# Attention pipeline on one core: full-array pieces and weighings in alternate slots, one double bank for the maxima

## What is computed

```python
def _L0_attn_ref(x, Wqkv, bqkv, Wout, bout):        # 16 heads of 8
    qkv = (x @ Wqkv + bqkv).reshape(B, S, 3, NUM_HEADS, HEAD_DIM)
    q, k, v = (qkv[0] * SCALE, qkv[1], qkv[2])      # after a transpose
    attn = jax.nn.softmax(jnp.einsum('bhqd,bhkd->bhqk', q, k), axis=-1)
    out = jnp.einsum('bhqk,bhkd->bhqd', attn, v)    # back to (B, S, D)
    return out @ Wout + bout

def step(c, xt):                                    # over the 16 images, in _L0_ffn_ref
    ft = jax.nn.sigmoid(xt @ wf.T + c @ uf.T + bf)
    it = jax.nn.sigmoid(xt @ wi.T + c @ ui.T + bi)
    gt = jnp.tanh(xt @ wc.T + c @ uc.T + bc)
    return ft * c + it * gt, None

x = x + _L0_attn_ref(_layernorm(x), ...)
x = x + _L0_ffn_ref(_layernorm(x), ...)
```

## Time and profile before

| what | us |
|---|---|
| median of the runs (three) | 636.96 |
| lowest and highest run | 636.06 and 641.02 |
| span of the profiled execution | 592.2 |
| its own time, taken at the median of the runs, so around the span | 44.8 |
| TensorE busy in the span | 490.3 (83%) |
| vector engine busy | 415.1 (70%) |
| ACT busy | 346.6 (59%) |
| GpSimd busy | 364.7 (62%) |

### The profile page before, as it was taken

One profiled execution on the slowest core, in us unless ns is written; L12 is line 12 of the kernel. 1 busy time (PEld: TensorE's weight loads), 2 busy tenths in 40 slices (PEclk: granted clock), 3 DMA queues, 4 the chain that ended last, 5 costly groups with the idle time before them and its releaser, 6 DMA issues. The chain is left out here.

```text
span 592.2 us, 14069 instructions
## 1 busy us (share of the span) xinstructions
PE 490.3 (83%) x4162; PEld 331.7 (56%) x4162; DVE 415.1 (70%) x1041; ACT 346.6 (59%) x749; POOL 364.7 (62%) x602
## 2 busy tenths in 40 slices
PE   4757889999999999998886899998657999888900
PEld 3423455555555555554463666666547898887800
DVE  6767878888888888784244899999856685454306
ACT  2026767777777777767723678887641565554500
POOL 3555677777777777534324158888764477777740
PEclk8769999999999999999999999998958899999955
DMA  3666435433343444210009999999921333333229
GB/s 106 166 170 190 128 87 128 109 85 101 98 105 110 110 112 109 83 36 4 2 2 317 379 376 365 367 366 366 329 63 53 93 86 96 95 90 89 76 80 353
DMA packets 78750, 90.00 MB, mean 152 GB/s; under 512 B 8395, under 2 KB 56032, under 8 KB 78688
## 3 DMA queue, kind: packets, MB, share of 16 engines
q1 hardware_dynamic: 72824, 79.67, 44.9%
q0 software_dynamic: 4576, 8.47, 4.3%
q10 hardware_dynamic: 1288, 1.11, 0.7%
HBM read 30.47 MB, written 59.72 MB: 152 GB/s over the span
## 5 line engine op out<-in xcount | busy, mean ns | idle before, releaser
L456 DVE TENSOR_REDUCE negmax<-p_dve 128x4 f32<-128x1024 f32 x128 | 156.2, 1223 | 46.9 <-PE p_dve L682 45.2
L574 ACT ACTIVATE probs<-p_exp 128x1024 f32<-128x1024 f32 x128 | 130.7, 1021 | 29.6 <-PE p_exp L656 28.8
L1606 POOL DMA_INDIRECT back<-XN2T,rows x79 | 82.6, 1045 | 36.8 <-issue 21.3
L1114 POOL DMA_INDIRECT disp<-pay,pos x64 | 65.3, 1021 | 18.1 <-issue 18.1
L673 PE MATMUL p_out<-probs,V 128*32 128x256 f32 x1024 | 75.2, 388 | 0.0
L656 PE MATMUL p_exp<-QS,KS 64*128 64x256 bf16 x512 | 50.6, 276 | 11.1 <-ACT probs L574 5.9
L682 PE MATMUL p_dve<-KS,QS 61*128 61x256 bf16 x512 | 51.2, 280 | 9.8 <-DVE negmax L456 9.7
L1731 ACT ACTIVATE hid<-p_qkv,own 128x128 f32<-128x128 f32 x150 | 42.8, 369 | 15.7 <-PE p_qkv L1769 15.4
L1661 DVE TENSOR_SCALAR own<-expert,every_bit 128x578 int32 x79 | 39.8, 545 | 8.4 <-issue 8.4
L1769 PE MATMUL p_qkv<-XN2T,own 128*128 128x128 f32 x316 | 43.2, 279 | 0.8 <-ACT XN2T L1705 0.8
L1122 POOL TENSOR_TENSOR roots<-roots,power 128x4 f32<-128x4 f32 x19 | 25.8, 1358 | 29.2 <-DVE roots L1318 28.7
(11 more groups left out here) (272 smaller groups left out, 1186.0 us busy)
## 6 DMA issues: line engine op xcount, KB each, us to landing
disp<-fill SPq DMA_DIRECT2D x8, 4160.0 KB, 38.1
scratch<-part SPq DMA_DIRECT2D x32, 192.0 KB, 2.1
KS<-scratch SPq DMA_DIRECT2D x32, 192.0 KB, 3.2
QS<-scratch SPq DMA_DIRECT2D x32, 192.0 KB, 4.3
rows<-disp SPq DMA_DIRECT2D x79, 65.0 KB, 1.8
scratch<-part SPq DMA_DIRECT2D x32, 128.0 KB, 1.9
own<-back SPq DMA_DIRECT2D x8, 512.0 KB, 6.9
expert<-in_W_dram SPq DMA_DIRECT2D x1, 2064.0 KB, 8.8
```

Source lines behind the costliest of these rows:

```text
L456: dve.tensor_reduce(negmax[q][:, i, :, 2 * hp:2 * hp + 2], p_dve[buf][:, :].rearrange("p (v w k) -> p v w k", v=HALF, k=S), AX.X, ALU.max, ...
L574: act.activation(probs[s % 4][:, :, :, :].rearrange("p v w q -> p (v w q)"), p_exp[:, :], ACT.Exp)\
L1114: pool.indirect_dma_start(out=disp, out_offset=bass.IndirectOffsetOnAxis(ap=pos[q][:, i, k:k + 1], axis=0), in_=pay[q][:, k, i, :], in_off ...
L1606: pool.indirect_dma_start(out=back, out_offset=bass.IndirectOffsetOnAxis(ap=rows[r][:, h, D + 1:ROW].bitcast(U32), axis=0), in_=y[r][:, h, :],
```

## The change

It does these things:

- Weighings come in pairs in slots 1, 3, 5 and 7 only; the last two of an image move from slot 0 to slot 1 of the next iteration.
- Full-array pieces stand in slots 0, 2, 4 and 6 only, in one function `whole_array`: slot 0 the turn of xn1 and V; slot 2 QK, the turn of the heads for all tokens, the turn of xn2; slot 4 the turn of `on`, the turn of the maxima, the candidate gate; slot 6 the output projection and the two gates.
- PSUM is laid out anew: all maxima go to one double bank `p_max`; the other double bank is cut in two, `p_tok` for V, the heads and the output projection, `p_cell` for xn2 and the candidate gate. Each maxima unit waits for the reduction of the unit before it.
- The vector engine does the quotient for all tokens in one pair of instructions in slot 2 and V's bias in slot 1. In the cell step the two waits change places.
- ACT copies `p_out` in slots 1 and 5, QK in slot 2, xn2 in slot 3, `on` in slot 4, and takes the tanh of the candidate gate in slot 5 and of the two gates in slot 7.

```diff
-WEIGHED_IN = {2: (0,), 3: (1,), 4: (2, 3), 6: (4,), 7: (5,)}
+WEIGHED_IN = {3: (0, 1), 5: (2, 3), 7: (4, 5)}
-DVE_BANK = (0, 1, 1, 1, 1, 0, 1, 1)
...
-        p_dve = [psum(f"p_dve{i}", 1024) for i in range(2)]
+        p_small = psum("p_small", 1024)
+        p_tok, p_cell = p_small[:, 0:512], p_small[:, 512:1024]
+        p_max = psum("p_max", 1024)
...
-                    if s in (1, 2) and active(n, 3):
-                        quotient(n - 3, s - 1)
-                    if s == 3 and active(n, 0):
+                    if s == 2 and active(n, 3):
+                        quotient(n - 3)
+                    if s == 1 and active(n, 0):
...
-                        if s == 4:
-                            copy_out(n - 2, (r - 2) % RING, 0)
-                    if s == 0 and active(n, 3):
-                        copy_out(n - 3, r, 1)
...
+                    if s == 1 and active(n, 3):
+                        copy_out(n - 3, r, 1)
+                    if s == 2 and active(n, -1):
...
+                        if active(n, 1):
+                            act.wait_ge(maxT_p.sem, maxT_p.at(n - 1))
...
+                    if s == 5 and active(n, 2):
+                        copy_out(n - 2, (r - 2) % RING, 0)
+                    if s == (5 if active(n, 2) else 7) and active(n, 4):
+                        b = n - 4
+                        act.wait_ge(gc_p.sem, gc_p.at(b))
+                        if cell.due(b - 1):
+                            act.wait_ge(cell.sem, cell.at(b - 1))
+                        act.activation(carry[:, 1, :], (p_cell if active(n, 2) else p_out)[:, 0:S], ACT.Tanh, bias=gates_b[:, 2:3]).then_inc(gc_s.sem, 1)
+                    if s == (7 if active(n, 2) else 5) and active(n, 4):
...
+            def turn_heads(n, r):
+
+                b = n - 3
+                pe.wait_ge(OT_s.sem, OT_s.at(b))
+                if active(n, 0):
+                    pe.wait_ge(v_s.sem, v_s.at(n))
+                elif active(n, 4):
+                    pe.wait_ge(x1_s.sem, x1_s.at(n - 4))
+                for i in range(TT):
+                    for side in range(SIDES):
+                        first = i * S + side * P
+                        turned_heads = p_tok[:, first:first + P].rearrange("p (l j c) -> p j l c", l=2, j=4)
+                        mm = pe.transpose(turned_heads, OT[r][:, side, i * P:(i + 1) * P], ident[:, :])
+                mm.then_inc(OQ_p.sem, 1)
...
+            def whole_array(n, r, s):
+
+                if s == 0:
                     if active(n, -1):
+                        turn_xn1(n, r)
+                    if active(n, 0):
+                        project_v(n, r)
+                elif s == 2:
+                    if active(n, -1):
+                        project_qk(n, r)
                     if active(n, 3):
+                        turn_heads(n, r)
+                    if active(n, 4):
+                        turn_xn2(n, r)
+                elif s == 4:
+                    if active(n, 3):
+                        turn_on(n, r)
                     if active(n, 1):
+                        turn_max(n)
+                    if active(n, 2) and active(n, 4):
+                        candidate(n, p_cell)
+                    if active(n, 3) and not active(n, 2):
+                        project_out(n, r)
+                elif s == 6:
...
+                    if active(n, 3) and active(n, 2):
+                        project_out(n, r)
+                    if active(n, 4):
+                        two_gates(n)
+                    if active(n, 4) and not active(n, 2):
+                        candidate(n, p_out)
...
-                        bank_free(n, s)
+                        if max_s.due(b, u):
+                            pe.wait_ge(max_s.sem, max_s.at(b, u))
...
-                        maxima(b, q, u, DVE_BANK[s])
-                    if s == 0 and active(n, 3):
+                        maxima(b, q, u)
+                    if s == 1 and active(n, 3):
                         weigh(n - 3, r, 6)
                         weigh(n - 3, r, 7)
...
+                    if s % 2 == 0:
+                        whole_array(n, r, s)
```

More of the change, by code:

```diff
@@ L631, in iteration @@
                                 .then_inc(gfi_s.sem, 1)
-                    if s == 7 and active(n, 4):
-                        b = n - 4
-                        act.wait_ge(gc_p.sem, gc_p.at(b))
-                        act.activation(carry[:, 1, :], (p_misc if active(n, 2) else p_out)[:, 0:S], ACT.Tanh, bias=gates_b[:, 2:3]).then_inc(gc_s.sem, 1)
             def copy_out(b, q, side):
@@ L675, in weigh, with maxima @@
                 mm.then_inc(pv_p.sem, 1)
[L677 removed]
+            def maxima(b, q, u):
                 i, hp = u // 4, u % 4
@@ new lines, in project_out, with candidate @@
+            def project_out(n, r):
+                pe.wait_ge(onT_s.sem, onT_s.at(n - 3))
+                if at(n, 3):
+                    pe.wait_ge(w_in.sem, w_in.at(0))
+                for i in range(TT):
+                    mm = pe.matmul(p_tok[:, i * P:(i + 1) * P], onT[:, i * P:(i + 1) * P], Wout[:, :], start=True, stop=True)
+                mm.then_inc(proj_p.sem, 1)
+            def candidate(n, bank):
+                b = n - 4
+                if cell.due(b - 1):
+                    pe.wait_ge(cell.sem, cell.at(b - 1))
+                else:
+                    pe.wait_ge(setup_done.sem, 4)
+                if active(n, 2):
+                    pe.wait_ge(xn2T_s.sem, xn2T_s.at(b))
+                else:
+                    pe.wait_ge(OT_s.sem, OT_s.at(B - 1))
+                pe.matmul(bank[:, 0:S], gates_w[:, 2, :], xn2T[:, :], start=True, stop=False)
+                pe.matmul(bank[:, 0:S], gates_uh[:, 2, :], state[:, :], start=False, stop=True).then_inc(gc_p.sem, 1)
@@ new lines, in two_gates @@
+            def two_gates(n):
+                b = n - 4
+                if active(n, 1):
+                    pe.wait_ge(maxT_s.sem, maxT_s.at(n - 1))
+                elif active(n, 2):
+                    pe.wait_ge(onT_s.sem, onT_s.at(n - 3))
+                else:
+                    pe.wait_ge(xn2T_s.sem, xn2T_s.at(b))
+                    pe.wait_ge(cell.sem, cell.at(b - 1))
+                for j in range(2):
+                    pe.matmul(p_misc[:, j * S:(j + 1) * S], gates_w[:, j, :], xn2T[:, :], start=True, stop=False)
+                    mm = pe.matmul(p_misc[:, j * S:(j + 1) * S], gates_uh[:, j, :], state[:, :], start=False, stop=True)
+                mm.then_inc(gfi_p.sem, 1)
```

256 lines of the change are left out of this document (87 added, 169 removed).

## The result

The changed kernel takes 645.76 us (median of four runs, 642.63 to 646.84), the kernel before 636.51 in the four runs beside it: ratio 1.0133, 95% interval 1.0082 to 1.0184. I had predicted 637.6 with 630.5 to 643.5. The change makes the kernel slower by 1.3%, and the time lies above the range.

What follows compares the result with a forecast made beforehand. It took TensorE to set the pace, except slots 0 to 2, a vector-engine chain. Fill +1.2, steady part +1.4 and drain -2.0 gave +0.6 on the 636.96 us median: 637.6 us, range 630.5 to 643.5.

Steps and rivals of the forecast that it cites:

- fill: Stretch up to 89 us: +2.6 at the first scores of image 0, net +1.2, bounds -1.5 and +4.
- steady part: Iterations 5 to 14: 16.26 us each instead of 16.12, +1.4 in all, bounds -3.4 and +4.4.
- drain: Last iterations, mostly without maxima: the regrouping pays up to ACT's limit, -2.0 us, bounds -4 and 0.
- it is won back in part: Fill, iterations 2 to 4: earlier maxima (about 0.5 and 0.3 us) and 0.6 more slack bring +2.6 to +1.2.
- the turn of the maxima in slot 4: TensorE, slot 4: about 0.13 us, taken as half a pair of turns because it is bf16.
- The main mechanism: One double bank: maxima wait for the previous reduction, 1.72 us apart in slots 3, 5, 7; slots 0 and 1 3.90.
- rival A: TensorE's switches decide and the single bank costs nothing: 623.1 us, chance 0.07; half of it, 632.8 us, chance 0.14.
- The holds' price: Steady iteration: TensorE's waits for reductions through the single bank cost 1.45 us.
- The cover of the quotient: Vector engine, slot 2: the quotient ends near 2.66, next maxima ready at 2.81, so hidden by 0.15 us.
- rival B: Slot 2's quotient of both halves delays the reduction behind it, 0.6 us per iteration: 643.6 us, chance 0.13.
- TensorE's own order: Steady iteration on TensorE if nobody else is late: 14.81 us, 1.3 below 16.12.
- Rival C: Fill at its upper bound because TensorE's low clock stretches maxima and QK: +2.8, 640.4 us, chance 0.10.

Runs made afterwards that it cites:

- e2: Changed kernel with each reduction reading only half of the keys; 580.03 us, steady iteration 15.21 us.
- e3: Kernel before the change with each reduction reading only half of the keys; 596.44 us, steady iteration 15.93 us.
- e5: Changed kernel with the maxima alternating between two double banks in iterations 0 to 2 only; 604.07 us.
- e6: Changed kernel with the turn of the maxima put first in slot 4; 604.7 us, steady iteration 16.31 us.
- e9: Changed kernel again, unaltered; 644.99 us (median of six), ratio 1.0158 to the kernel before.
- e8: Changed kernel with the edits of e5 and e6, the cell step's second instruction moved to slot 1, slot 7's maxima in the other double bank; 590.27 us.
- e10: Same code as e8, against the kernel before; 630.09 us (median of six), ratio 0.990.
- e1: Kernel before the change again, unaltered; 593.54 us.
- e11: Kernel before the change with only the cell step's second instruction moved to slot 1; 638.08 us (median of twelve), ratio 1.0037.
- e7: Changed kernel with 19 matmuls on the identity added in the last iteration's waits; 608.22 us.

## Why the prediction was wrong

The forecast was +0.6, of three terms: fill +1.2, steady part +1.4, drain -2.0. They measured +5.3, +3.9 and +1.8. The step that failed most is in the fill, "it is won back in part": between the first scores and iteration 5 nothing is won back, 1.5 us more are lost. In the steady part a size was off, the turn of the maxima in slot 4. In the drain a lower clock, for which the sum has no term, took more than the new order gave.

**The main mechanism was right.** The single bank puts TensorE on the vector engine's chain of 1.72 us in slots 0, 5 and 7 and leaves M(0) to M(2) at 3.9. e2 and e3 show it against rival A, which fell: with the chain out of the way the iteration is 15.21, not 16.50. The Trainium skill's rule ("Perfetto Trace Analysis", Optimizing Tensor Performance, Matmuls) that independent matmul groups should rotate through PSUM banks is borne out: e5 gives the fill its second bank back, and from the first maxima to the first scores it takes 21.60 instead of 23.65. The holds' price comes from e2: 1.28 per iteration; I had put it at 1.45.

**Steady part, +1.4 predicted, +3.9 measured.** Slot by slot, predicted and measured: M(0) to M(2) 3.90, 3.91; slot 2 2.38, 2.26; slot 3 1.72, 1.81; slot 4 1.91, 2.20; slots 5, 6, 7 1.72, 2.91, 1.72, then 1.71, 2.93, 1.70. The mis-sized term is slot 4: I took "about 0.13 (half a pair, it is bf16)" for the turn of the maxima, which no row of mine showed. It adds 0.22 for itself and 0.1 in each of the pieces around it, 0.42 in all; e6 took 0.19 of that away by order alone. The cover of the quotient, 0.15 by my sum, was in truth -0.11. It started at M(2) + 1.92 (I had 1.97), but the reduction behind it started only at + 2.79: 0.40 from the start of the reciprocal and 0.47 from that of the product to the next. The maxima of slot 3 could have been reduced at + 2.26 + 0.42. This is rival B in kind, but with 0.09 us for slot 3, not 0.6, and in six of the ten iterations only. TensorE's own order was put at 14.81; e2 shows 15.21. Slot 4 is 0.28 of the difference, slot 0 another 0.23: its turn starts 0.50 behind the maxima there, as I had said, which the 1.72 was to hide and does hide in the changed kernel. Slot 2 gives 0.12 back.

**Fill, +1.2 predicted, +5.3 measured.** This is the largest miss and lies outside its own bounds (-1.5 to +4). Up to the first scores I had +2.6; in e9, whose first maxima start where they did before, it is 44.30 - 41.67 = +2.6. That is luck. Of my 2.6, 0.5 was V ahead of the first maxima, and these start no later in e9 (20.66 against 20.67). The chain behind them costs 2.65 (23.65 against 21.00) where I had 2.1. "1.72 to 1.9 each" was too short: at the low clock it is 1.93 from the fifth unit on. And the count that matters is the thirteen units up to the first scores and not the eight of image 0: I had followed the last reduction of image 0 and "a fixed distance" behind it, but the scores stand behind M(7) of the same iteration on TensorE, and that was the later of the two.

The step that failed is the next one, "it is won back in part". Iteration 2 grew by 2.2 us (17.54 against 15.34; 18.86 in e9) instead of falling by 0.5. Its first 8.6 us run at the lower clock, while before the change the clock was back from 46 us on:

```profile
45.45:54.00 8.55, 6.94 (x38) 3.51 (x38) 5.23 (x5) 3.47 (x5) 0.91 (x3) 0.50 0.97 250
```

How long the clock stays low isn't fixed by the kernel either: iteration 2 took 17.95 in e8 and 16.06 in e10, of one code, with the clock low until about 52 and 46 us. Iterations 3 and 4 did win 0.3 and 0.4 (14.38 and 16.91 against 14.72 and 17.27). e2 and e3 leave little for V and QK by themselves: with short reductions both orders reach iteration 5 at 88.3. e5 shows 3.1 of the 5.3 to go with the second bank, e8 and e10 2.0 and 4.6. What is left is the longer stretch at the low clock and the wait for V that e5 brought; no run separates these, and whether the one bank also keeps the clock low longer stays open.

**Drain, -2.0 predicted, +1.8 measured.** The order itself gains less than I put: iteration 15 +0.06 (predicted -0.2), iteration 16 -0.4 (predicted -0.8; of the 0.4 missing, 0.3 is slot 4 again, 1.97 from scores to scores where I had 1.68), and the rest -0.8 where the clock stayed at 1.00 (28.37 in e8, 29.18 before; predicted -1.0): -1.2 together. The granted clock then cost 2.9 in the profiled execution (1.6 in e9). I had no term for it, since the profile before had 1.00 there.

**Rival C** had the right place and sign, and its mechanism, the low clock that stretches the maxima, is in the rows; its upper bound of 2.8 more was too small, 4.1 came. It alone would not have carried the time out of the range: the steady part and the drain added 2.5 and 3.8.

## What to carry to other kernels

When two buffers of a pipeline are merged into one, the price is not only the hold in each slot but everything that stands between two uses on the other engine; list these pieces first, and see whether one can move to a slot with room (0.46 us here per iteration from one instruction, but a loss of 0.14 in the kernel before, where the slot had none). Count the fill separately, with the durations at the clock that the fill has, and over every unit that stands ahead of the first useful instruction on its engine. Look how far two profiles of one kernel agree in a stretch before you explain a difference there: the steady iterations of the changed kernel repeat to 0.01 us, the start of the maxima, iteration 2 and the end of the stage differ by 1 to 2 us. And keep two buffers where the bank is idle anyway, as the fill and one slot allowed here.

## What the runs showed of the hardware that I had not expected

- Slot 4 with the bf16 turn between two fp32 pieces goes 0.32 + 0.37 + 0.22 + 0.54 from start to start on TensorE; with that turn behind the bf16 maxima it goes 0.33 + 0.22 + 0.27 + 0.44, about 0.2 less. The Trainium skill ("TensorEngine Tiling (Array Packing)", Key Properties) says that a change of tiling mode drains TensorE; here fewer changes were a gain, but the type changed along with the tiling, and no run parts the two.
- The granted clock at the end of the stage was 1.00, 0.89 or 0.80 for the same instructions, 13.74, 15.34 and 16.70 us.
- The part behind the stage, of one code, takes 280 to 288 us in the first profile and on the chips of e1 to e8, and 321 to 326 in the profile after and on the chip of e9 to e11, with 212 GB/s moved in the first profile and 185 after, and a granted clock of 0.90 and 0.86. Which of the two makes the time, if either, no run shows. The steady iterations agree on all of them: 16.11 and 16.11 before, 16.50 in all four profiles of the changed kernel's steady part (after, e5, e7, e9). An absolute time from one chip is not to be set beside one from another; a stage's may be, once a run of the same kernel has shown that it repeats.
